# State-space stage of a hybrid block: decays as exponentials of running-sum differences, loop unrolled into overlapping periods

## The reference, cut to what matters

```python
zxbcdt = layernorm(x) @ W_in                   # z 256 | x, B, C 512 | dt 4 columns
xBC = silu(conv(xBC, 4 taps) + conv_b)         # causal, by channel
x, Bm, Cm = xBC[:256] as 4 heads of 64, 128 states, 128 states
dt = softplus(dt + dt_bias);  dA = dt * -exp(A_log)          # by token and head
# in chunks of 32 tokens, with the state carried from chunk to chunk:
y[i] = sum over j <= i of (C_i . B_j) * exp(sum of dA over j+1..i) * dt_j * x_j
y = (y + x * D) * silu(z)
y = y * rsqrt(mean(y * y) + 1e-5) * norm_w
x = x + y @ W_out
```

## Time and profile before

| | us |
|---|---|
| median of three runs | 1010.67 (1010.19 to 1013.47) |
| profiled execution | 1009.58 |
| its span | 1007.8 |
| attention and first FFN | 0 to 452 |
| state-space stage | 452.0 to 906.8 |
| second FFN | 907 to 1007.8 |
| busy over the span: PE, DVE, ACT, POOL | 867.0, 760.7, 465.6, 415.2 |

### The profile page before, as it was taken

The page is one execution under the profiler, slowest core; times in us unless marked ns, Lnnn a source line. Parts: engine busy times, 40 slices in busy tenths (PEclk is TensorE's granted clock), DMA queues, the critical chain, the costliest instruction groups (busy, mean ns, idle before and its releaser), DMA issues.

```text
span 1007.8 us, 18069 instructions
## 1 busy us (share of the span) xinstructions
PE 867.0 (86%) x5410; PEld 665.4 (66%) x5410; DVE 760.7 (75%) x2030; ACT 465.6 (46%) x911; POOL 415.2 (41%) x748
## 2 busy tenths in 40 slices
PE   2589999999998789997878797878889797879998
PEld 1478888888886657774646465555556464656776
DVE  1467877777785377767898998989888989947885
ACT  2234343443433467765434344534444353426775
POOL 0456666666664022111434443534435344442121
PEclk9579999999999999997979798999979899988999
DMA  8322121211212000000000000000000000000112
GB/s 227 78 51 57 47 61 37 70 38 47 61 36 49 12 1 0 0 2 0 1 1 1 0 0 0 0 0 0 0 0 0 0 0 0 0 1 22 42 42 63
DMA packets 75026, 26.35 MB, mean 26 GB/s; under 512 B 29536, under 2 KB 74720, under 8 KB 74976
## 3 DMA queue, kind: packets, MB, share of 16 engines
q1 hardware_dynamic: 74976, 25.72, 10.0%
HBM read 15.23 MB, written 10.49 MB: 26 GB/s over the span
## 4 chain that ended last, share of the span: by engine, by line
PE 52%; issue 21%; DVE 8%; POOL 7%; ACT 4%; DMA 3%; POOLq 0%; ACTq 0%; DVEq 0%; SPq 0%
PE bank L1379 9%; PE bank L1359 4%; PE bank L1358 4%; PE bank L1424 3%; POOL arena L525 3%; PE bank L1200 3%; PE bank L1470 2%; PE bank L1539 2%; DMA ff<-T_dram 2%; PE bank L1524 2%; PE bank L1288 2%; PE bank L1193 2%; PE bank L1275 2%; PE bank L1256 2%; PE bank L1175 1%
## 5 line engine op out<-in xcount | busy, mean ns | idle before, releaser
L525 POOL TENSOR_TENSOR arena<-arena 128x768 f32<-128x768 f32 x64 | 115.4, 1807 | 155.6 <-DVE arena L1044 77.9
L1044 DVE TENSOR_TENSOR_SCAN arena<-bank,tab 128x256 f32<-128x256 f32 (+1 forms) x256 | 121.1, 534 | 33.6 <-PE bank L1458 32.5
L1034 DVE SCALAR_TENSOR_TENSOR arena<-bank,convw_sb,arena 128x510 f32<-128x510 f32 (+2 forms) x192 | 135.3, 732 | 1.5 <-ACT arena L688 1.5
L448 POOL TENSOR_TENSOR var_eps<-mv,eps_cols 128x4 f32<-128x4 f32 x66 | 13.1, 199 | 254.1 <-DVE mv L765 189.8
L1470 PE MATMUL bank<-arena 128*64 128x256 f32 x256 | 88.8, 432 | 29.2 <-POOL arena L525 29.2
L1379 PEld LDWEIGHTS bank<-downT,ff 128*128 128x128 f32 x768 | 89.5, 192 | 8.8 <-DVE ff L961 6.4
L1379 PE MATMUL bank<-downT,ff 128*128 128x128 f32 x768 | 91.3, 275 | 2.4 <-DVE ff L961 2.4
L659 ACT ACTIVATE ff<-bank 128x512 f32<-128x512 f32 x96 | 56.8, 591 | 58.2 <-PE bank L1359 58.2
L694 ACT ACTIVATE arena<-arena 128x512 f32<-128x512 f32 x64 | 39.8, 622 | 92.2 <-DVE arena L1034 92.1
L562 ACT ACTIVATE xn<-x_all,shift,rstd 128x128 f32 (+1 forms) x192 | 78.5, 481 | 0.1
L1424 PE MATMUL bank<-xnT,win_sb 128*128 128x512 f32 x128 | 72.2, 670 | 1.6 <-DVE arena L1034 1.6
(11 more groups left out here) (166 smaller groups left out, 2023.3 us busy)
## 6 DMA issues: line engine op xcount, KB each, us to landing
LT_dram<-arena SPq DMA_DIRECT2D x16, 256.0 KB, 2.3
ff<-T_dram SPq DMA_DIRECT2D x16, 256.0 KB, 3.0
ff<-R_dram SPq DMA_DIRECT2D x16, 256.0 KB, 3.3
out<-x_all SPq DMA_DIRECT2D x8, 512.0 KB, 3.2
x_all<-in_L_attn_a_x SPq DMA_DIRECT2D x7, 512.0 KB, 7.3
x_all<-in_L_attn_a_x SPq DMA_DIRECT2D x2, 256.0 KB, 3.3
T_dram<-tab SPq DMA_DIRECT2D x2, 256.0 KB, 2.7
R_dram<-tab SPq DMA_DIRECT2D x2, 256.0 KB, 3.3
```

Source lines behind the costliest of these rows:

```text
L525: nc.gpsimd.tensor_tensor(score[h % 2][u], cb[u], hgam[h % 2][u], ALU.mult).then_inc(score_done[u], 1)
L1034: nc.vector.scalar_tensor_tensor(acc, src, convw_sb[:, q, TAPS - 1 - s:TAPS - s], acc, ALU.mult, ALU.add).then_inc(tap_done[v], 1)
L1044: last = nc.vector.tensor_tensor_scan(hgam[h % 2][u][:, strip(b, c)], bank[u][(3, 0)[h % 2]][:, b * SEQ + c * P:(b + 1) * SEQ], eye_zero[: ...
```

## The change

The groups no longer go in pairs in a loop. The stage is written out as 18 periods h = 0..17, in which `space_half` does the front of group b = h, the middle of group e = h - 1 (scores and head outputs), and the output (W_out, mean, residual) of group f = h - 2. The layer norm runs 7 groups ahead, the projection of dt 6 groups ahead; those of groups 2 to 6, and the first chain, stand in a stretch ahead of period 0. The chain of dt runs once per four groups (a quad), with its stages in four successive periods. At its end the running sums, 32 rows of 256 tokens, are split into three f16 pieces, written to DRAM by SP and read back eight times as rows of two operands.

The logarithm of a decay is then a difference of two sums, made on PE in a bank that first takes a mask (`never16`, -30000 above the diagonal) and then products with 6 rows of pieces (`log_decay`, six f16 matmuls a head). ACT takes the exponential of two batches of 384 columns a head (`decay_of`): the scans on DVE and the transposes of broadcast columns on PE are gone. ACT loads its function table twice in each period. There are now four score buffers, and `head_outputs(r)` makes two heads with their products alternating between the two halves of PE's columns. POOL adds the two squares, so that the sum of squares takes half the matmuls; POOL also sets rows of constants in the stretch ahead.

```diff
+XNT_SETS = 8
+QUAD = 4
+LN_LEAD, DT_LEAD = 7, 6
...
+        z_dt, dt_dt = ([sb(f"dt_{n}{k}", [P, QCOLS]) for k in range(2)] for n in ("z", "dt"))
+        flat_ff = [ff[u][:, :, :].rearrange("p k c -> p (k c)") for u in U]
+        from_rows, to_rows = ([flat_ff[u][:, k * 2 * GROUP:(k + 1) * 2 * GROUP].bitcast(f16) for u in U] for k in range(2))
...
+        pieces = sb("pieces", [QROWS, PIECES, SEQ], f16)
...
+        conv_bank, mid_bank, step_bank, y_bank = bank[0][0:2], bank[0][2:4], bank[1][0:2], bank[1][2:4]
...
+        def ssd_ln(h):
+            g = h + LN_LEAD
+            if LN_LEAD <= g < GROUPS:
+                return 2 * GROUPS + g, g % XNT_SETS
+            return (3 * GROUPS + h - GROUPS + 1, h - GROUPS + 1) if GROUPS - 1 <= h <= GROUPS else None
+        def ssd_half(h):
+            return ssd_group(h), ssd_group(h - 1), ssd_group(h - 2), ssd_ln(h), ssd_group(h + DT_LEAD)
...
+        def quad_at(h, stage):
+            q, left = divmod(h - stage + QUAD - 1, QUAD)
+            return q if left == 0 and 1 <= q < GROUPS // QUAD else None
...
+            for q in range(GROUPS // QUAD):
+                side = q % 2
+                sp.wait_ge(chain_step, CHAIN * (q + 1))
...
+                sp.dma_start(pieces_dram[side].rearrange("m r c -> r m c"), pieces[:, :, :]).then_inc(pieces_out, 16)
+                sp.wait_ge(pieces_out, 16 * (q + 1))
+                sp.wait_ge(rows_set, 4)
+                sp.wait_ge(E_mm, past(2 * HEADS * QUAD * (q - 1) - 1))
+                for j in range(QUAD):
+                    src = pieces_dram[side][:, j * BATCHES * HEADS:(j + 1) * BATCHES * HEADS, :].rearrange("m r c -> m (r c)")
+                    sp.dma_start(from_rows[side][32 * j:32 * j + 2 * PIECES:2, :], src).then_inc(pieces_in, 16)
+                    sp.dma_start(to_rows[side][32 * j + 1:32 * j + 1 + 2 * PIECES:2, :], src).then_inc(pieces_in, 16)
...
+            def space_half(b, e, f, x, d):
+                if x is not None:
+                    ln_rstd_of(*x)
+                if f is not None:
+                    pool.wait_ge(ms_done, done(f))
+                    nc.gpsimd.tensor_tensor(rms[f % 2], ms[f % 2], half_neg[:, :], ALU.pow).then_inc(rms_done, 1)
+                if e is not None:
                     for h in range(HEADS):
...
+                        pool.wait_ge(hgam_done, done(2 * HEADS * e + 2 * h + 1))
+                        pool.wait_ge(cb_done, done(BATCHES * e + 1))
+                        pool.wait_ge(hy_mm, past(INNER_BLOCKS * (e - 1) + h // 2))
+                        nc.gpsimd.tensor_tensor(score[h], cb[e % 2], hgam[h], ALU.mult).then_inc(score_done, 1)
                     for r in range(INNER_BLOCKS):
...
+                        pool.wait_ge(ydt_done, done(INNER_BLOCKS * e + r))
+                        pool.wait_ge(sz_done, done(INNER_BLOCKS * e + 1))
+                        nc.gpsimd.tensor_tensor(yT[r][e % 2], yT[r][e % 2], siluz[r][e % 2], ALU.mult).then_inc(yT_done, 1)
+                    pool.wait_ge(ysq_done, done(INNER_BLOCKS * e + 1))
+                    nc.gpsimd.tensor_tensor(ysq[0][e % 2], ysq[0][e % 2], ysq[1][e % 2], ALU.add).then_inc(ysum_done, 1)
...
+                def decay_of(h):
+                    for batch in range(BATCHES):
+                        act.wait_ge(E_mm, done(2 * HEADS * e + 2 * h + batch))
+                        act.wait_ge(score_done, past(HEADS * (e - 1) + h))
+                        nc.scalar.activation(hgam[h][:, batch * TRI:(batch + 1) * TRI], step_bank[batch][:, 0:TRI],
+                                             ACT.Exp).then_inc(hgam_done, 1)
+                if e is not None:
+                    silu_x(e, 2)
+                    silu_x(e, 3)
+                if b is not None:
                     first_tap(0)
                     first_tap(1)
+                if e is not None:
+                    for batch in range(BATCHES):
...
+                    for h in range(HEADS):
+                        decay_of(h)
+                if quad is not None:
+                    exp_of_quad(quad)
+                if b is not None:
                     first_tap(2)
...
                     first_tap(3)
...
+                begin_q, end_q, sums_q, split_q = quads
+                if x is not None:
+                    stats_at(*x)
+                if split_q is not None:
+                    split_sums(split_q)
+                if b is not None:
+                    for s in range(1, TAPS):
+                        taps(s, 0, 1)
+                if f is not None:
...
+                if x is not None:
+                    shift_at(*x)
+                if sums_q is not None:
+                    running_sums(sums_q)
+                if end_q is not None:
+                    softplus_middle(end_q)
+                if b is not None:
+                    taps(1, 2, 3)
+                if f is not None:
+                    add_residual(f)
+                if b is not None:
+                    taps(2, 2, 3)
+                if end_q is not None:
+                    softplus_end(end_q)
+                if e is not None:
                     skip(0)
...
+                if b is not None:
                     times_dt(0)
                     times_dt(1)
...
+                    taps(3, 2, 3)
+                if d is not None:
+                    with_bias(d)
+                if end_q is not None:
+                    chunk_sums(end_q)
+                if begin_q is not None:
+                    softplus_begin(begin_q)
+                if e is not None:
+                    skip(1)
...
+                def log_decay(h):
+                    j, side = e % QUAD, e // QUAD % 2
+                    rows = slice(32 * j, 32 * j + 2 * PIECES)
+                    for batch in range(BATCHES):
+                        to = step_bank[batch]
+                        a = (batch * HEADS + h) * SEQ
+                        pe.wait_ge(hgam_done, past(2 * HEADS * e + 2 * h + batch - 2))
+                        mm(to[:, 0:TRI], ident16[:, :], never16[:, :], start=True, stop=False)
+                        mm(to[:, 0:SEQ], from_rows[side][rows, a:a + P], to_rows[side][rows, a:a + SEQ],
+                           start=False, stop=False)
+                        mm(to[:, SEQ:TRI], from_rows[side][rows, a + P:a + SEQ], to_rows[side][rows, a + P:a + SEQ],
+                           start=False, stop=True).then_inc(E_mm, 1)
+                def head_outputs(r):
+                    pe.wait_ge(score_done, done(HEADS * e + 2 * r + 1))
+                    if r == 0:
+                        pe.wait_ge(x_done, past(2 * GROUPS + e - 1))
+                        pe.wait_ge(xt_done, done(INNER_BLOCKS * e + 1))
+                    else:
+                        pe.wait_ge(ms_done, past(e - 1))
+                    x_of = tile4(xt[e % 2])
+                    for batch in range(BATCHES):
+                        for c in range(2):
+                            for k in range(2):
+                                h = 2 * r + k
+                                last = mm(y_bank[r][k * HEAD_DIM:(k + 1) * HEAD_DIM, batch * SEQ + c * P:(batch + 1) * SEQ],
+                                          x_of[:, 2 * batch + c, h * HEAD_DIM:(h + 1) * HEAD_DIM], score[h][:, strip(batch, c)],
+                                          start=(c == 0), stop=(c == 1))
+                    last.then_inc(hy_mm, 1)
...
+                if b is not None:
+                    pe.wait_ge(xnT_done, done(2 * GROUPS + b))
                     conv(0)
                     conv(1)
...
+                if e is not None:
+                    products(0)
+                    products(1)
+                    pe.wait_ge(pieces_in, 16 * 2 * QUAD * (e // QUAD + 1))
+                    log_decay(0)
+                if f is not None:
+                    pe.wait_ge(ysum_done, done(f))
...
+                if e is not None:
+                    log_decay(1)
+                if f is not None:
+                    pe.wait_ge(yT_done, done(INNER_BLOCKS * f + 1))
...
+                if e is not None:
+                    log_decay(2)
+                if b is not None:
                     conv(2)
...
                     conv(3)
+                if e is not None:
+                    log_decay(3)
+                if b is not None:
                     gate(0)
+                    gate(1)
+                if e is not None:
+                    head_outputs(0)
+                if b is not None:
                     token_major(0)
                     token_major(1)
...
+                if x is not None:
...
+                    transposes_of(*x, mid_bank[0])
+                if d is not None:
+                    pe.wait_ge(xt_done, done(INNER_BLOCKS * b + 1))
+                    of_token(d)
+                if quad is not None:
+                    pe.wait_ge(xt_done, done(INNER_BLOCKS * b + 1))
+                    steps_to_rows(quad)
+                if e is not None:
+                    head_outputs(1)
```

670 lines of the change are left out of this document (320 added, 350 removed).

## The result

| | before | after |
|---|---|---|
| median | 1010.43 us of 4 runs (1007.45 to 1013.47) | 1050.97 us of 4 (1048.24 to 1053.51) |
| ratio | | 1.0401, 95% interval 1.0356 to 1.0445 |
| span of the profiled execution | 1007.8 | 1046.4 |
| state-space stage, from the end of the first FFN's last add | 451.1 to 906.8: 455.8 | 452.9 to 945.5: 492.6 |
| end of the first residual adds, behind the stage's start | 47.2 | 100.3 |

The account below looks back on a forecast made before the run. No engine full: a loop of hand-overs, DVE heaviest, bounds the stage. First residual 86, 8 steps 213, chains 6, five steps 126, end 32: 463 against 454.8, +8 on 1009.6, median 1019; own range 1006 to 1040, stated 985 to 1054.

Parts of the forecast that it names:

- rival A: Head outputs on PE: the halves of PE's columns don't overlap, +2.9 us a period, +36, 1055 us; chance .15.
- The loop of one period: State-space stage, from one period's second head outputs to the next: 25.5 us at full clock, 26.6 with the clock, against 27.7.
- Log-decays: PE's products for a batch of log-decays: .33 plus two changes of shape at .09, .51 us, eight a group 4.1.
- Exponentials: ACT's exponentials of 384 columns read from PSUM: .49 us each, as a copy of 384; eight are 3.9.
- Head outputs: PE's products for two heads, alternating between column halves with full overlap: 1.45 us, against 2.8 without overlap.
- Table load: ACT's function table loads: 1.28 us each with no drain ahead, two a period 2.6, against one a group before.
- The clock: PE's granted clock of .90 in the stage: 11% more on 10.4 us of PE terms, +1.1 us a period.
- The time to the first residual: Start of the stage: 30 us ahead of period 0, periods 19 and 22, period 2's residual after 14, +1 clock: 86.
- the fills: Four f16 fills by POOL, which with the extra tables' loads lie beside work and cost 0 to 2 us.
- The end: End of the stage: the last two steps, without fronts, take 32 us.
- B: Stage clock: PE's long wait goes and the clock stays near full; 1000 us, between 993 and 1004; chance .27.
- C: Whole stage: slack decouples the engines, PE alone sets a period of 21.5 us, −46, 965 us; chance .06.

Follow-up runs that it names:

- e2: Kernel after, with ScalarE's first taps of blocks 2 and 3 moved between the exponentials of heads 2 and 3; 1028.1 us, ratio 1.0102 to the kernel before.
- e5: Kernel after, with the square of a group's second half moved behind the next period's two SiLUs and first taps; 1023.9 us, ratio 1.0144 to the kernel before.
- e3: Kernel after, with the decays taking SiLU in place of Exp, so no table is loaded for them (other values); 1024.1 us, ratio 1.0145 to the kernel before.
- e8: Kernel after, with log-decays made of 128-row products in place of 6-row ones, so no change of shape (decays 0 or 1); 1010.2 us, ratio 0.9991.
- e4: Kernel after, with 24 unread f16 products added per period, ahead of C·B's products and the first head outputs; 1039.9 us, ratio 1.0274 to the kernel before.
- e12: e11 with six unread f16 products of 384 columns added behind each sum of squares; 987.9 us, ratio 0.9784 to the kernel before.
- e1: Kernel after, with the stretch ahead of period 0 reordered: statistics and shifts before group 2's bias, first Exp and constant fills later; 1041.9 us, ratio 1.031.
- e7: Kernel after, with each head's four products together instead of alternating between the halves of PE's columns; 1067.7 us, ratio 1.0495 to the kernel before.
- e6: Kernel after, with e1, e2 and e5 together and the first chain's sums and split moved behind period 0's first six taps; 987.9 us, ratio 0.9753.
- e11: e6 with both masks of a head put ahead of the pieces and a one-column Exp ahead of the C·B copies; 1000.4 us, ratio 0.9869.

## Why the forecast was right, and where its sizes were off

The direction and its reason held: PE, ACT and DVE form one loop of hand-overs, the 8.5 us of scans of the earlier trace rows were not its bound, and the start costs more than the steps give back. The forecast was 1019 and the result 1051. That is outside the forecast's own range, 1006 to 1040; the stated range of 985 to 1054 holds it only because it had taken in the lower half of rival A, whose mechanism did not occur. So the direction was earned, and that the range held was in part luck. Three of the signs named ahead failed: the first residual at 86 us (101), a clock of .88 to .93 (.85 over the stage) and steps of 26 to 27 us (28.0 for the first eight, with the chains of dt). By the steps of the sum:

- **The loop of one period**, 26.6 with layer norm, 25.2 without: measured 28.0 with the chains of dt (forecast 27.4), and 26.1. Its links were as drawn. Two of them were tested by order alone (e2, e5), with gains of 23 and 27 us, and a third by leaving the table loads out (e3), 27 us.
- **Log-decays** .51, measured .53; the change of shape .09, measured .10 (e8). **Exponentials** .49, measured 490 ns a piece. **Head outputs** 1.45, measured 1.45 to the next start. **Table load** 1.28 with no drain: trace and e3 agree.
- **The clock** is the term of the period that was mis-sized. I had the average of the stage before, .90, on 10.4 us of PE: 1.1 a period. Two things were wrong. The average fell to .85. And the low level is not spread: in the period shown it lies on C·B and W_out, just as PE becomes the engine that ACT waits for, 3.4 us in a step of 26.2. Without it that step would be 22.8, where the forecast's loop has 24.1 at full clock, so the other terms together were 1.3 too long and hid part of this miss (an estimate: it takes all 3.4 as lying on the path). By a count of levels, 2 × (1 − .85) × 493 = 148 us of the stage are at 1.2 GHz against 2 × (1 − .90) × 455 = 91 before; if PE were always late that is 28 us more lost than before (an estimate, an upper bound by construction). Why the average fell is shown in part: e4 and e12 raise it by products in pauses and behind the short ones, e8 by having no 6-row products.
- **The time to the first residual**, 86 from 452.0, is the largest miss: 101.3. PE's timeline in after gives the parts. L1578 opens a period; L1659 and the last row belong to period 2.

```profile
484.97 3.39 PE L1578 MATMUL bank<-xnT,win_sb 128*128 128x512 f32 x4 [0.85 <-issue]
...
505.53 1.96 PE L1578 MATMUL bank<-xnT,win_sb 128*128 128x512 f32 x4
...
529.08 1.98 PE L1578 MATMUL bank<-xnT,win_sb 128*128 128x512 f32 x4
...
538.07 2.90 PE L1659 MATMUL bank<-wout_sb,arena 128*128 128x128 f32 x16
...
542.50 3.65 PE L1578 MATMUL bank<-xnT,win_sb 128*128 128x512 f32 x4
```

The stretch ahead is 33.0 for 30, period 0 20.6 for 19, period 1 23.6 for 22, and period 2 takes 24.2 to the end of its residual adds where I had 14. That 14 contradicts the forecast's own loop, whose first five lines up to the residual are 2.8 + 5.2 + 6.6 + 2.5 + 1.85 = 19.0: 5 of the 10 are a slip of the sum, and some 3 came with the low clock on W_out, log-decays and two convolutions (3.5 to the next start for 1.8). Of the 3.0 in the stretch ahead 1.9 lie ahead of the stage itself. Its clock is .61, at which a projection of dt takes 1.7 for .9, and GpSimd's fills of constants hold up DVE's series. Timelines of GpSimd and DVE in after:

```profile
472.52 3.75 POOL L578 CAST ff<-tab 128x2048 f16<-128x2048 f32 x2
...
472.72 1.79 DVE L1130 SCALAR_TENSOR_TENSOR dt_acc<-dt_acc,dt_w 128x64 f32<-128x64 f32 x1
474.55 1.80 DVE L1130 SCALAR_TENSOR_TENSOR dt_acc<-dt_acc,dt_w 128x64 f32<-128x64 f32 x1
476.38 1.00 DVE L1130 SCALAR_TENSOR_TENSOR dt_acc<-dt_acc,dt_w 128x64 f32<-128x64 f32 x4
```

and in e1, where no fill lies beside the same six:

```profile
479.75 1.52 DVE L1129 SCALAR_TENSOR_TENSOR dt_acc<-dt_acc,dt_w 128x64 f32<-128x64 f32 x6
```

I had put the fills at 0 to 2 as work that lies beside. The series of six takes 4.66 (472.72 to 477.38) and 1.52 in e1, so they cost it 3.1. DVE isn't slower throughout: two operations last until the fill under which they started ends, and four take their usual .23. The earlier trace rows show the same once (DVE's 1.43 from 668.68 ends with GpSimd's 1.80 from 668.26, at 670.1); I knew the collision and did not look for a second one.

- **The end**, two steps without fronts at 32: measured 37.8, at a clock of .78.

The sum of the misses: +15 to the first residual, +5 and +5 for the steps, +6 for the end, 31 with rounding, is the whole difference from 452.0 on (463 to 493.5). The median stands 2.7 over the profiled execution and not 1.1, which makes the 32 of 1019 to 1051.

Of the rivals, A ended nearest, 1055, by a mechanism that did not occur: the halves do overlap (e7). B had the sign of the clock wrong: it had PE's long waits gone and the clock near full, and PE still waits up to 4.3 us and the clock fell; its own sum is off too, 1001 less 8 being 993 and not 1000. C would need ACT's order to let go; with e6's moves the steps fall to 23.0 on average, near C's 21.5, with PE busy 307 of 346 us at a clock of .88. That is the way to C's bound and no proof of it, since DVE and ACT still wait on each other in e6.

## What to carry to other kernels

When work leaves the busiest engine, walk the loop of waits before counting the gain, and use that same loop for the periods at the start. Then look at each engine's queue for an instruction that waits for a late result ahead of one whose input is long there: two such (a square, two first taps) were worth 50 us here, more than the 40 that the change cost. Price the start of a deeper pipeline by itself: a first result 53 us later is three times what 15 steps give back. And an average granted clock is no price: ask which products run behind a pause or a light stretch of PE. Here those ran at half speed, and they were the ones that others waited for.

## What the runs showed of the hardware

- The clock can fall without a long pause: in e6 it is .50 for 9 us in which PE has no pause at all, behind 3.5 us of short f16 products, changes of shape and waits of .2 to .5. In after it also falls behind a wait of 2.3 us. Adding products that nobody reads made two kernels faster (e4 by 11 us against after, e12 by 9 to 12 against e11).
- The same program's time mostly follows its clock from run to run: 22 us in e2 for .022 of the mean clock, 22 in e11 for .033. It is no rule: in e1 the two runs at the higher clocks (.919 and .917) are 4 us slower than those at .913 and .910.
- Going from 128 rows to 6 and back between f16 products costs .10 us each way (.53 for a batch of three products, .33 without the changes).
- Halves of PE's columns that alternate take .09 a pass (1.45 for 16 passes of 256 and 128 columns, which one after the other would need 2.6 by the forecast's prices), and with heads in turn 2.12.
- A small DVE operation that starts while GpSimd casts 2048 columns can last until the cast ends: 1.8 us for .2, twice in after and three times in e1. The others of the six in after take .23 each.
